# Conditioned transformer layer: value products of two key tiles at a time, four places for the probabilities, Wq and Wk resident by halves

## The chip, the cores and the metric

The kernel runs on one core of one Trainium2 chip, in one launch. The metric is device time in microseconds (us) of that core. TensorE (PE in the profile) multiplies matrices, VectorE (DVE), ScalarE (ACT) and GpSimd (POOL) work on elements, SyncE (SP) issues most transfers. Products land in eight PSUM banks of 128 x 512 floats, all else lies in SBUF.

## What is computed

```python
x = x + layer(x, cond)         # x: (4, 1024, 512) f32, cond: (4, 128)
def layer(x, t):               # 16 heads of 32
    x = x + attention(rmsnorm(x, t, g1, b1), Wq, Wk, Wv, Wo)
    return x + swiglu(rmsnorm(x, t, g2, b2), gate_w, hid_w, out_w)
def rmsnorm(x, t, gw, gb, bw, bb):
    g = (t @ gw.T + gb)[:, None, :]; b = (t @ bw.T + bb)[:, None, :]
    return g * x * rsqrt(mean(x * x, -1) + 1e-6) + b
def attention(x, Wq, Wk, Wv, Wo):
    p = softmax(einsum('blhd,bmhd->bhlm', q, k) / sqrt(32))
    return einsum('bhlm,bmhd->blhd', p, v).reshape(B, L, D) @ Wo.T
```

All is float32 in and out.

## The kernel before

`attention_program` (L241) runs first, for the four batches one after the other, then `ffn_program` (L1183) for the four. Each returns one function per engine; the engines meet only at semaphores. The change is in attention; of the feed-forward part it touches the places of tiles alone.

**Precision.** Most products are made of three with rounded parts (`product3_part`, L924): high x high, high x low, low x high. The probabilities times the values, and the denominators, are full float32 products. They have 32 columns of weights per head, so the four heads of a group run side by side in the array, and each is two instructions: a group of four heads is a row "x8" in the timeline.

**Stages of a batch.** The value stage (L1082) makes V for the eight token tiles, with the first projections and maxima woven in. Then come NU = 8 units: unit u treats head group g = u // 2 (four heads) and query half u % 2 (512 queries). In a unit TensorE goes through NS = 8 key tiles s and GH = 4 heads h; I write (s, h), or q = 4 s + h. At each (s, h) it makes one tile of scores (L1107) into one of three banks, one product for the row maxima of the next unit but a few (`max_tile`, L992, three banks, reduced by VectorE at L754), and what a table adds: a quarter of a Q or K projection (PROJECTED, L36 to L42, `project`, L958), a turned token tile of the next batch (HT_AT), the maxima's rows (MAXIMA_AT), the denominators (SUMS_AT, L46) and the values (VALUES_AT, L50). Last, eight output tiles (`out_tile`, L1019).

**The probabilities.** ScalarE writes exp of the scores (L658) to `probs`, which has places for two key tiles, s % 2. Two engines read them:

```python
46  SUMS_AT = {(5, 1): (0, 0), (1, 1): (1, 1)}
50  VALUES_AT = (3, 1, 3, 2)
498                     total = sum_place(s // QT, h)
499                     first = probs[:, 0, h, :] if s % QT == 1 else total
1123                        if h == VALUES_AT[s % QT] and (u or s):
1124                            values(b, u if s else u - 1, (s - 1) % NS)
```

GpSimd adds up each quad of four key tiles (L486 to L501): nothing at s % 4 == 0, then four sums for each of the other three tiles, in order, 24 a unit. `denominators` (L1006) on TensorE then adds over the partitions: at (5, 1) for the unit's first quad, at (1, 1) of the next unit for the second. It waits until the quad's sums are done, and GpSimd's sum at (s % 4 == 1, h = 1) waits until the denominators before it have read the places (L494). GpSimd also does the normalisation of the unit before, ahead of s = 5 (`normalise`, L460), and at (3, 6) and (6, 3) an inverse root for the next batch's norm (L456).

`values` (L1038) multiplies one key tile, four heads, and adds to the bank `obank`: tile s - 1 at (s, h) with h from VALUES_AT. The places bind ScalarE: at each s it waits until the values of tile s - 2 are done (L644), and except at s % 4 == 3 until GpSimd has taken up tile s - 2 (L654). After (0, 3) ScalarE copies the finished unit out (`output`, L582).

**The weights.** Wq, Wk (high and low part each) and Wo's low part stay in SBUF, 2048 floats per partition each. Wv's parts lie under `probs` and come back from DRAM for every batch; ScalarE issues that (L687) after the last denominators. Their rounding and splitting, `weight_hi` and `weight_lo`, is done in the lead-in on VectorE (L796 to L803), Wv's and Wo's rounding on ScalarE (L613). VectorE's splitting of Wo (L844) stands ahead of its first maxima.

**SP's queue** (L346 to L441) is in order: lead-in loads, the copies of Q and K parts stacked for the products ("stacking", 12 transfers a tile, L354), stores of Wv's and Wo's parts (L396, L398) with a wait for the latter (L399), then per unit the stackings, loads of x and of Wo.

Of the kernel before, what the change touches and what calls it, by code (L numbers as in the profile page):

```python
# [11 lines left out]
P = 128  # L12
# [37 lines left out]
VALUES_AT = (3, 1, 3, 2)  # L50
# [190 lines left out]
def attention_program(nc, ctx, x, cond_small, cond_in, W_in, attn, wv_dram, wo_dram, W, cst, psum):  # L241
# [10 lines left out]
    probs = at("probs", [P, 2, GH, QB], F32, "probs")  # L252
# [25 lines left out]
    raw = [at("wq_raw", [P, KT, D], F32, "wq_lo"), at("wk_raw", [P, KT, D], F32, "wk_lo"),  # L278
           at("wv_raw", [P, KT, D], F32, "probs_lo"), at("wo_raw", [P, KT, D], F32, "wo_lo")]
    split = [W[0], W[1], [wv[:, 0, :, :], wv[:, 1, :, :]], [wo[0], wo[1]]]  # L280
# [18 lines left out]
    wv_stored = sem("wv_stored")  # L299
    wo_stored = sem("wo_stored")  # L300
# [45 lines left out]
    def sync_part(sp, lead):  # L346
# [44 lines left out]
        sp.sem_inc(wv_loaded, 16)  # L391
# [6 lines left out]
        sp.dma_start(wo_dram, wo[0][:].bitcast(F32)).then_inc(wo_stored, 16)  # L398
        hold(sp, held, wo_stored, 16)  # L399
        def batch(b):  # L400
# [5 lines left out]
            for u in range(NU):  # L406
# [37 lines left out]
    def gpsimd_part(pool):  # L444
# [24 lines left out]
        def batch(b):  # L469
            last = isinstance(b, int)  # L470
            for u in range(NU):
                for s in range(NS):
# [13 lines left out]
                    for h in range(GH if s % QT else 0):  # L486
# [12 lines left out]
                        first = probs[:, 0, h, :] if s % QT == 1 else total  # L499
                        nc.gpsimd.tensor_tensor(total, first, probs[:, s % 2, h, :], ALU.add) \  # L500
# [7 lines left out]
    def scalar_part(act, lead):  # L508
# [104 lines left out]
        def weight_hi(w):  # L613
            act.wait_ge(w_loaded[w], 16)
            nc.scalar.activation(split[w][0][:], raw[w][:], ACT.Copy).then_inc(w_hi[w], 1)
# [11 lines left out]
        def batch(b):  # L627
            last = isinstance(b, int)
            for t in range(NT):

                act.wait_ge(st_ready, SCORES_T(b, t + 1))
                if t == 0:

                    act.wait_ge(pv_done, b * (NU * NS) + 2)
# [5 lines left out]
            for u in range(NU):  # L640
                for s in range(NS):
                    n = u * NS + s

                    act.wait_ge(pv_done, b * (NU * NS) + n + 1)  # L644
# [3 lines left out]
                    if u == 0 and s == 0:  # L648

                        act.wait_ge(wv_stored, 16)  # L650
                    for h in range(GH):
# [1307 lines left out]
```

## Time and profile before

| | |
|---|---|
| runs of the kernel | 2383.4 us median of 3 (2380.82 to 2390.84) |
| profiled execution, span of its instructions | 2384.2 us |
| the profiled execution's own time | not recorded beside its span |
| attention, four batches | to about 1372 us |
| units 0 to 7 of batch 1 | 427.85 to 701.37 us |
| TensorE, VectorE, ScalarE, GpSimd busy | 96%, 70%, 54%, 60% of the span |
| granted TensorE clock, mean | 0.989 of full speed |

The page is one profiled execution. Busy time of an engine is the time in which one of its instructions ran. Matmuls are pipelined: a row's duration overlaps the next row's, so that the distance of starts is what one costs. "Idle before <-X" says that the engine waited and whose instruction ended the wait.

### The profile page before, as it was taken

What the parts mean: (1) busy time and instruction counts of PE and PEld (TensorE: products, weight loads), DVE (VectorE), ACT (ScalarE), POOL (GpSimd) and SP (SyncE); (2) the same over time, 40 slices, a digit from 0 to 9 for tenths busy, and PEclk for the clock granted to TensorE, in tenths of its full rate; (3) what the DMA queues carried; (4) which work ended last, traced back from release to release, by engine and by line L of the source; (5) the groups of instructions that cost most, each with busy time, mean ns of one, the idle gap of its engine ahead of it and who ended that gap; (6) DMA issues with size and microseconds to landing.
All of it is one profiled execution on the core that took longest, in us unless ns stands there. A gap on an engine that the chain in (4) does not pass through costs nothing.

```text
span 2384.2 us, 38858 instructions
## 1 busy us (share of the span) xinstructions
PE 2279.8 (96%) x10848; PEld 1561.5 (65%) x10848; DVE 1658.1 (70%) x2719; ACT 1284.7 (54%) x2286; POOL 1421.4 (60%) x1331
## 2 busy tenths in 40 slices
PE   6899999999999999999999889999999999999998
PEld 5555447555457554465554468887888788888887
DVE  4777754677736777546777378877887788778877
ACT  3366672567762666735666654363436344544354
POOL 0299891699961898925999837504760466036701
PEclk9899999999999999999999999999999999999999
DMA  5321213222132222132221232046114621363125
GB/s 163 99 66 33 66 32 112 52 60 54 49 94 59 53 47 72 32 111 46 48 54 32 106 133 62 27 151 221 54 36 133 204 81 36 106 200 113 44 89 177
DMA packets 91333, 203.06 MB, mean 85 GB/s; under 512 B 15200, under 2 KB 15200, under 8 KB 89440
## 3 DMA queue, kind: packets, MB, share of 16 engines
q1 hardware_dynamic: 90672, 194.06, 27.4%
q10 hardware_dynamic: 432, 6.29, 0.7%
q8 instruction: 102, 1.67, 0.3%
q14 instruction: 127, 1.04, 0.1%
HBM read 130.03 MB, written 19.92 MB: 63 GB/s over the span
## 4 chain that ended last, share of the span: by engine, by line
PE 80%; DVE 6%; issue 5%; ACT 4%; DMA 2%; POOL 2%; SPq 2%; DVEq 0%; ACTq 0%; POOLq 0%
PE bank L1814 26%; PE bank L1828 12%; PE bank L927 10%; PE bank L1107 9%; PE bank L1046 8%; PE bank L1002 8%; PE bank L1033 3%; PE bank L1012 2%; POOL sums L500 1%; DVE pmax L754 1%; ACT probs L658 1%; SPq L365 1%; PE bank L988 1%; DMA wo_raw<-in_out_w 1%; DVE ow L1634 1%
## 5 line engine op out<-in xcount | busy, mean ns | idle before, releaser
L754 DVE TENSOR_REDUCE pmax<-bank 128x1 f32<-128x512 f32 x1024 | 651.9, 683 | 210.0 <-PE bank L1002 202.0
L658 ACT ACTIVATE probs<-bank 128x512 f32<-128x512 f32 x1024 | 566.2, 602 | 304.6 <-PE bank L1107 253.7
L500 POOL TENSOR_TENSOR sums<-sums,probs 128x512 f32<-128x512 f32 x432 | 540.7, 1287 | 0.0
L1107 PE MATMUL bank<-qs,ks 128*128 128x512 f32 x1024 | 435.6, 430 | 12.1 <-ACT probs L658 9.7
L1002 PE MATMUL bank<-ks,qs 96*128 96x512 f32 x1024 | 407.2, 410 | 30.0 <-DVE pmax L754 29.0
L1107 PEld LDWEIGHTS bank<-qs,ks 128*128 128x128 f32 x1024 | 192.7, 189 | 276.0 <-issue 130.7
L1828 PE MATMUL bank<-ow,aw 128*128 128x512 f32 x1536 | 360.8, 392 | 3.1 <-DVE ow L1634 3.0
L1814 PE MATMUL bank<-H_hi,wt_hi 128*128 128x512 f32 x896 | 350.6, 391 | 8.6 <-DVE H_lo L1669 8.3
L1814 PE MATMUL bank<-H_hi,wt_lo 128*128 128x512 f32 x896 | 350.1, 391 | 0.0
L1814 PE MATMUL bank<-H_lo,wt_hi 128*128 128x512 f32 x896 | 350.0, 391 | 0.0
L1828 PEld LDWEIGHTS bank<-ow,aw 128*128 128x128 f32 x1536 | 285.0, 188 | 65.7 <-issue 6.7
L500 POOL TENSOR_TENSOR sums<-probs 128x512 f32<-128x512 f32 x224 | 282.9, 1283 | 55.3 <-ACT probs L658 50.8
L1046 PE MATMUL bank<-probs,v 128*32 128x512 f32 x2048 | 275.1, 609 | 2.7 <-ACT probs L658 2.7
L1392 POOL TENSOR_TENSOR wt_lo<-s_ring,wt_hi 128x256 fp32r<-128x256 f32 x224 | 185.1, 859 | 151.6 <-ACT wt_hi L1459 151.6
L1002 PEld LDWEIGHTS bank<-ks,qs 96*128 96x128 f32 x1024 | 194.6, 190 | 101.3 <-DVE pmax L754 68.9
L500 POOL TENSOR_TENSOR yout<-probs 128x512 f32<-128x512 f32 x32 | 41.0, 1280 | 305.7 <-ACT probs L658 305.7
L1814 PEld LDWEIGHTS bank<-H_hi,wt_hi 128*128 128x128 f32 x896 | 169.0, 189 | 46.6 <-ACT a L1547 6.9
L1814 PEld LDWEIGHTS bank<-H_hi,wt_lo 128*128 128x128 f32 x896 | 168.9, 189 | 35.2
L1814 PEld LDWEIGHTS bank<-H_lo,wt_hi 128*128 128x128 f32 x896 | 168.9, 189 | 35.1
L1453 ACT ACTIVATE wt_hi<-raw 128x512 fp32r<-128x512 f32 x65 | 41.0, 631 | 262.7 <-PE bank L1814 262.1
L1377 POOL TENSOR_TENSOR s<-raw 128x256 f32<-128x256 f32 x9 | 7.8, 867 | 288.5 <-DVE aw L1629 288.5
L1492 ACT ACTIVATE aw<-a 128x512 fp32r<-128x512 f32 x128 | 80.4, 628 | 108.2 <-PE bank L1828 93.6
(181 smaller groups left out, 3321.4 us busy)
## 6 DMA issues: line engine op xcount, KB each, us to landing
raw<-in_gu_w SPq DMA_DIRECT2D x66, 512.0 KB, 3.6
wo_raw<-in_out_w SPq DMA_DIRECT2D x128, 256.0 KB, 2.8
qs<-qk_hi SPq DMA_DIRECT2D x256, 64.0 KB, 2.0
ks<-qk_hi SPq DMA_DIRECT2D x128, 128.0 KB, 2.4
x<-attn_out SPq DMA_DIRECT2D x10, 1024.0 KB, 8.5
x<-in_x SPq DMA_DIRECT2D x8, 1024.0 KB, 5.1
qs<-qk_lo SPq DMA_DIRECT2D x128, 64.0 KB, 2.0
ks<-qk_lo SPq DMA_DIRECT2D x64, 128.0 KB, 2.4
```

The source lines that it names most:

```text
L500: nc.gpsimd.tensor_tensor(total, first, probs[:, s % 2, h, :], ALU.add) \
L658: nc.scalar.activation(probs[:, s % 2, h, :], sbank[i % SB][:], ACT.Exp, scale=SCALE).then_inc(st_done, 1)
L754: nc.vector.reduce_max(pmax[:, t, h, hf:hf + 1], mbank[n % MB][:], AX_X).then_inc(sq_done, 1)
L927: last = nc.tensor.matmul(out, lhs(a, k), rhs(c, k), start=(k == 0 and a == 0 and c == 0), stop=(k == kdim - 1 and a == 1))
L1002: nc.tensor.matmul(mbank[n % MB][:], qs[0:96, u % 3, h, t * P:(t + 1) * P], ks[0:96, u // 2 % 2, h, hf * QB:(hf + 1) * QB], start=True, st ...
L1033: last = nc.tensor.matmul(bank[:], osplit[:, t % 2, a, k, :], wo[c][:, k, :], start=(k == 0 and a == 0 and c == 0), stop=(k == NG - 1 and ...
L1046: last = nc.tensor.matmul(obank[DH * h:DH * h + DH, :], v[:, s, (g * GH + h) * DH:(g * GH + h + 1) * DH], probs[:, s % 2, h, :], start=(s ...
L1107: nc.tensor.matmul(sbank[i % SB][:], ks[:, g % 2, h, s * P:(s + 1) * P], qs[:, u % 3, h, :], start=True, stop=True).then_inc(st_ready, 1)
L1392: nc.gpsimd.tensor_tensor(lo[:, S1 + i], src[:, i], hi[:, S1 + i].bitcast(F32), ALU.subtract).then_inc(s_lo, 1)
L1492: nc.scalar.activation(aw[n % 3][:, 0, :], a[:, j, blk, :], ACT.Copy).then_inc(a_hi, 1)
L1814: last = nc.tensor.matmul(bank[:], wt[j % 2][p][:, weight, i, :], H[q][:, h, i, :], start=(i == 0 and p == 0 and q == 0), stop=(i == 1 and ...
L1828: last = nc.tensor.matmul(psum[4 * blk + t][:], aw[n % 3][:, p, t * P:(t + 1) * P], ow[n % 3][:, q, :], start=(j == 0 and p == 0 and q == ...
```

## The change

1. The values of two key tiles are multiplied in one go, four times a unit: tiles 0 and 1 at (3, 1), 2 and 3 at (5, 1), 4 and 5 at (7, 1), 6 and 7 at (1, 1) of the next unit, there and at (5, 1) right behind the denominators.
2. `probs` has four places, s % 4. ScalarE waits for values only at even s, for the pair two before, and for sums four tiles back. `output` moves from (0, 3) to (1, 1), the copying of the first denominators from (5, 2) to (5, 1).
3. The space for that: Wq and Wk are held for two of four head groups. The lead-in splits groups 0 and 1 first, 2 and 3 later (into space that the probabilities use afterwards), and SP stores all parts to DRAM. In each batch SP reloads each group over one that is done with (`load_group`, eight loads of 512 KB, six of them placed by unit; in the last batch only the four of units 0 and 1). Projections wait for the loads.
4. Wv's reload is issued by ScalarE after the last exponential instead of after the last denominators.
5. Places of some feed-forward tiles are exchanged.

```diff
-VALUES_AT = (3, 1, 3, 2)
+PAIRS = NS // 2
+VALUES_AT = {(3, 1): (0, 0), (5, 1): (0, 1), (7, 1): (0, 2), (1, 1): (1, 3)}
...
+    def probs(s, h):
+        return probs_parts[s % 4 // 2][:, s % 2, h, :]
...
+        def load_group(b, kind, g):
+
+            last_user = ("Q", 2 * g + 1) if kind == "Q" else ("K", 2 * g, NHALF - 1)
+            to, dram, loaded = (wq, wq_dram, wq_loaded) if kind == "Q" else (wk, wk_dram, wk_loaded)
+            hold(sp, held, w_ready, MISC(b, 0 if last_user == ("K", 0, NHALF - 1) else misc_index(b, last_user) + 1))
+            hold(sp, held, loaded, b * (NG * 16) + 16 * (g + 1))
+            sp.dma_start(to[:, g % 2, :, :, :].bitcast(F32), dram[(g + 2) % NG]).then_inc(loaded, 16)
...
         hold(sp, held, w_hi[3], 1)
         sp.dma_start(wo_dram, wo[0][:].bitcast(F32)).then_inc(wo_stored, 16)
+        for w, (dram, lower) in enumerate(((wq_dram, wq), (wk_dram, wk))):
+            for half, part in enumerate((lower, upper[w])):
+                hold(sp, held, w_lo[w], half + 1)
+                sp.dma_start(dram[2 * half:2 * half + 2].rearrange("g p a k c -> p g a k c"),
+                             part[:].bitcast(F32)).then_inc(qk_stored, 16)
         hold(sp, held, wo_stored, 16)
...
                     stack(b, ("Q", u + 2), (u + 2) % 3)
+                if u == 0:
+                    hold(sp, held, qk_stored, 64)
+                    load_group(b, "Q", 0)
+                    load_group(b, "K", 0)
+                elif u == 1:
+                    load_group(b, "Q", 1)
+                    load_group(b, "K", 1)
+                elif u < 6 and not last:
+                    load_group(b, "K" if u % 2 == 0 else "Q", u // 2 + 1)
...
-                    act.wait_ge(pv_done, b * (NU * NS) + n + 1)
+                    if s % 2 == 0:
+                        act.wait_ge(pv_done, b * (NU * PAIRS) + n // 2 + 1)
...
-                        if s % QT != QT - 1:
-
-                            act.wait_ge(sum_done, sums_done(b, u, s - 2, h) if s >= 2
-                                        else sums_done(b, u - 1, NS + s - 2, h))
-                        nc.scalar.activation(probs[:, s % 2, h, :], sbank[i % SB][:], ACT.Exp,
+                        if s % QT != 1:
+
+                            act.wait_ge(sum_done, sums_done(b, u, s - QT, h) if s >= QT
+                                        else sums_done(b, u - 1, NS + s - QT, h))
+                        nc.scalar.activation(probs(s, h), sbank[i % SB][:], ACT.Exp,
...
-                        if (s, h) == (5, 2):
+                        if (s, h) == (5, 1):
                             work_tile(b, ("D", u, 0))
...
-                        if (s, h) == (0, GH - 1) and u:
+                        if (s, h) == (1, 1) and u:
                             output(b, u - 1)
...
+                        if (u, s, h) == (NU - 1, NS - 1, GH - 1) and not last:
+
+                            act.wait_ge(pv_done, b * (NU * PAIRS) + NU * PAIRS + 1)
+                            act.wait_ge(sum_done, sums_done(b, u, 5, GH - 1))
+                            act.dma_start(wv[:].bitcast(F32), wv_dram).then_inc(wv_loaded, 16)
...
         for hf in range(NHALF):
             work_tile(None, ("K", 0, hf))
+        for w in range(2):
+            weight_hi(w, 1)
+            weight_lo(w, 1)
         weight_lo(3)
...
-        def values(b, u, s):
+        def values(b, u, pair):
 
             g = u // 2
-            pe.wait_ge(st_done, SCORES_T(b, NT + (u * NS + s + 1) * GH) + SB)
-            if s == 0:
+            pe.wait_ge(st_done, SCORES_T(b, NT + (u * NS + 2 * pair + 2) * GH) + SB)
+            if pair == 0:
 
                 pe.wait_ge(od_act, b * NU + (u + 1))
-            for h in range(GH):
-                last = nc.tensor.matmul(obank[DH * h:DH * h + DH, :], v[:, s, (g * GH + h) * DH:(g * GH + h + 1) * DH],
-                                        probs[:, s % 2, h, :], start=(s == 0), stop=(s == NS - 1))
+            for s in (2 * pair, 2 * pair + 1):
+                for h in range(GH):
+                    last = nc.tensor.matmul(obank[DH * h:DH * h + DH, :], v[:, s, (g * GH + h) * DH:(g * GH + h + 1) * DH],
+                                            probs(s, h), start=(s == 0), stop=(s == NS - 1))
             last.then_inc(pv_done, 1)
...
                         if sums_at(u, s, h):
                             denominators(b, *sums_at(u, s, h)[1:])
-                        if h == VALUES_AT[s % QT] and (u or s):
-                            values(b, u if s else u - 1, (s - 1) % NS)
-            values(b, NU - 1, NS - 1)
+                        back, pair = VALUES_AT.get((s, h), (NU, 0))
+                        if u >= back:
+                            values(b, u - back, pair)
+            values(b, NU - 1, PAIRS - 1)
```

## Rows read from the trace of the kernel before

**Rows 1.** The page, part 5, the largest group of sums on GpSimd (POOL)

```profile
L500 POOL TENSOR_TENSOR sums<-sums,probs 128x512 f32<-128x512 f32 x432 | 540.7, 1287 | 0.0
```

**Rows 2.** Timeline of TensorE, batch 3, into unit 6: start, us, what, [idle before <-releaser]

```profile
1290.00 0.40 PE L1002 MATMUL bank<-ks,qs 96*128 96x512 f32 x1
1290.33 1.06 PE L1046 MATMUL bank<-probs,v 128*32 128x512 f32 x8
1291.33 0.50 PE L1107 MATMUL bank<-qs,ks 128*128 128x512 f32 x1
1291.66 0.40 PE L1002 MATMUL bank<-ks,qs 96*128 96x512 f32 x1
...
1292.14 0.40 PE L1002 MATMUL bank<-ks,qs 96*128 96x512 f32 x1
1294.11 1.06 PE L1012 MATMUL bank<-sums,ones 128*32 128x512 f32 x8 [1.57 <-POOL sums L500]
1294.96 1.07 PE L1046 MATMUL bank<-probs,v 128*32 128x512 f32 x8
1295.96 0.50 PE L1107 MATMUL bank<-qs,ks 128*128 128x512 f32 x1
```

**Rows 3.** Timeline of GpSimd over the same stretch

```profile
1293.91 1.28 POOL L500 TENSOR_TENSOR yout<-probs 128x512 f32<-128x512 f32 x1
...
1297.17 2.52 POOL L500 TENSOR_TENSOR sums<-probs 128x512 f32<-128x512 f32 x2 [0.55 <-ACT probs L658]
```

**Rows 4.** By stage, batch 1: length, PE, PEld, DVE, ACT, POOL busy, clock, DMA

```profile
427.85:452.07 24.22, 23.30 (x108) 13.79 (x106) 17.75 (x28) 13.71 (x25) 15.02 (x13) 1.00 0.36 79
452.07:469.59 17.52, 17.28 (x90) 9.39 (x90) 12.44 (x24) 12.06 (x22) 14.92 (x12) 1.00 0.12 29
469.59:485.65 16.06, 16.06 (x85) 8.84 (x84) 12.85 (x22) 9.24 (x19) 15.43 (x13) 1.00 0.41 115
485.65:502.56 16.91, 16.82 (x89) 9.26 (x88) 11.51 (x22) 12.28 (x23) 15.72 (x13) 1.00 0.00 1
502.56:519.49 16.93, 16.59 (x86) 8.83 (x85) 12.92 (x22) 9.26 (x19) 16.23 (x13) 1.00 0.49 107
...
552.47:569.41 16.94, 16.85 (x89) 9.27 (x89) 12.07 (x25) 12.76 (x24) 16.73 (x14) 1.00 0.00 0
569.41:588.31 18.90, 17.45 (x89) 9.12 (x88) 13.58 (x23) 12.93 (x25) 16.21 (x13) 1.00 0.54 120
...
605.23:621.88 16.65, 15.39 (x85) 7.78 (x85) 13.84 (x24) 12.30 (x24) 16.02 (x13) 1.00 0.39 108
621.88:637.51 15.63, 14.12 (x78) 6.98 (x77) 11.50 (x22) 12.80 (x25) 15.17 (x14) 1.00 0.20 71
637.51:654.40 16.89, 16.42 (x85) 8.74 (x85) 12.15 (x21) 10.35 (x23) 16.20 (x14) 1.00 0.01 2
654.40:670.43 16.03, 12.99 (x77) 6.12 (x77) 4.78 (x11) 15.19 (x28) 15.83 (x13) 1.00 0.13 30
670.43:689.33 18.90, 17.87 (x94) 9.89 (x93) 6.92 (x11) 15.84 (x30) 15.31 (x13) 1.00 0.16 36
689.33:701.37 12.04, 11.35 (x67) 5.74 (x70) 1.29 (x2) 7.47 (x14) 9.77 (x8) 1.00 0.47 104
...
898.66:918.56 19.90, 18.74 (x89) 9.55 (x88) 13.57 (x23) 12.96 (x25) 16.25 (x14) 0.91 0.54 120
```

**Rows 5.** Timelines of VectorE, SyncE and TensorE in the lead-in and first value stage

```profile
19.61 1.22 DVE L798 CAST wk_hi<-wk_raw 128x2048 fp32r<-128x2048 f32 x1
...
62.95 0.32 SPq L398 DMA_DIRECT2D wo_part<-wo_hi  x1
...
66.43 1.39 PE L1002 MATMUL bank<-ks,qs 96*128 96x512 f32 x2 [13.97 <-DVE pmax L754]
...
83.80 0.39 PE L927 MATMUL bank<-hT_hi,wk_hi 128*128 128x512 f32 x1
```

**Rows 6.** The DMA issues by line: KB each, median us from issue to landing

```profile
wv_parts<-wv SPq DMA_DIRECT2D x1, 2048.0 KB, 11.2
```

More of the change, by code:

```diff
@@ L277, in attention_program, with split, whole @@
     gwT = at("gwT", [P, 4, D], F32, "cond_w")
-    raw = [at("wq_raw", [P, KT, D], F32, "wq_lo"), at("wk_raw", [P, KT, D], F32, "wk_lo"),
+    raw = [at("wq_raw", [P, NG, KT, P], F32, "sums"), at("wk_raw", [P, NG, KT, P], F32, "o_up"),
            at("wv_raw", [P, KT, D], F32, "probs_lo"), at("wo_raw", [P, KT, D], F32, "wo_lo")]
-    split = [W[0], W[1], [wv[:, 0, :, :], wv[:, 1, :, :]], [wo[0], wo[1]]]
+    upper = [at("wq_up", [P, 2, 2, KT, P], F32R, "probs_up"), at("wk_up", [P, 2, 2, KT, P], F32R, "wk_up")]
+    def split(w, part, half):
+        if w < 2:
+            return ((wq, wk)[w] if half == 0 else upper[w])[:, :, part, :, :]
+        return (wv[:, part, :, :], wo[part][:])[w - 2]
+    def whole(w, half):
+        return raw[w][:, 2 * half:2 * half + 2, :, :] if w < 2 else raw[w][:]
     sbank = psum[0:SB]
@@ L650, in batch @@
                         act.wait_ge(wv_stored, 16)
+                    if u == 0 and s == 2:
+                        act.wait_ge(qk_stored, 64)
                     for h in range(GH):
@@ L969, in project @@
             g = tile[1] // 2 % NG
+            if b is not None and k == 0 and tile != ("Q", 1):
+                order = NG if tile[1] == NU else g
+                pe.wait_ge(wq_loaded if tile[0] == "Q" else wk_loaded, b * (NG * 16) + order * 16)
             hf = tile[1] % 2 if tile[0] == "Q" else tile[2]
-            product3_part(work_bank(b, tile)[:], lambda a, k: w[a][:, k, g * P:(g + 1) * P],
+            product3_part(work_bank(b, tile)[:], lambda a, k: w[:, g % 2, a, k, :],
                           lambda c, k: hT[c][:, k, hf * QB:(hf + 1) * QB], k, KT, w_ready)
@@ L1014, in denominators @@
             for h in range(GH if direct else 0):
-                last = nc.tensor.matmul(wbank[DH * h:DH * h + DH, :], ones[:], probs[:, (NS - 1) % 2, h, :], start=False,
+                last = nc.tensor.matmul(wbank[DH * h:DH * h + DH, :], ones[:], probs(NS - 1, h), start=False,
                                         stop=True)
@@ L1844, in condition_block @@
     wo_dram = nc.dram_tensor("wo_part", (P, KT, D), F32, kind="Internal").ap()
+    wq_dram, wk_dram = (nc.dram_tensor(f"{n}_parts", (NG, P, 2, KT, P), F32, kind="Internal").ap() for n in ("wq", "wk"))
     base = (nc.sbuf_base + 31) // 32 * 32
-    WEIGHTS = ("wq_hi", "wq_lo", "wk_hi", "wk_lo", "wo_lo")
     def plan(start, regions):
@@ L1858, in condition_block @@
     const_at, base = plan(base, small)
[L1859 removed]
+    weights_at, after_weights = plan(base, [("wq", KT * D), ("wk", KT * D), ("wo_lo", KT * D), ("probs_up", 2 * GH * QB)])
     attention_at, _ = plan(after_weights, [
@@ L1890, in condition_block @@
     cst["g1"], cst["b1"], cst["g2"], cst["b2"] = cst["cond"]
-    parts = [at(n, [P, KT, D], F32R, n) for n in WEIGHTS]
-    W = [parts[0:2], parts[2:4], parts[4]]
+    W = [at(n, [P, 2, 2, KT, P], F32R, n) for n in ("wq", "wk")] + [at("wo_lo", [P, KT, D], F32R, "wo_lo")]
     with ExitStack() as ctx:
         psum = [ctx.enter_context(nc.psum_tensor(f"bank{i}", [P, QB], F32)) for i in range(8)]
-        attention, ends = attention_program(nc, ctx, x, cond_small, cond_w, w_in, attn, wv_dram, wo_dram, W, cst, psum)
+        attention, ends = attention_program(nc, ctx, x, cond_small, cond_w, w_in, attn, wv_dram, wo_dram, wq_dram, wk_dram, W, cst, psum)
         ffn = ffn_program(nc, ctx, x, attn, gu_w, out_w, out, ends, cst, psum)
```

47 lines of the change are left out of this document (26 added, 21 removed).

## The prediction, made before the changed kernel was run

> **What bounds the kernel now.** I read the page's busy shares first: TensorE is busy 96% of the 2384.2 us span, and no other engine is over 70% (the table above). That is a mean over two programs. The change touches only the first, attention (to about 1.37 ms), so I cut one batch of it into stages. In program order the natural cut is the pair of points in each unit where TensorE issues the denominators' products (`denominators`, L1006): head 1 of key tile 1 and of key tile 5. I call the stretch from one such start to the next a half: A ends at tile 5, B at tile 1 of the next unit, and each has 16 scores. The table by stage of batch 1 [rows 4] gives a length, the busy time of each engine and the granted clock for every half.
>
> The reader is to see two things there. First, most halves are nearly full on TensorE: 16.06 of 16.06 us busy in A of units 1 and 3, 16.8 of 16.9 in B of units 1, 2 and 4. Second, GpSimd is not the relaxed engine that its 60% suggests. It is busy 14.9 to 16.7 us in each half but the last, and from unit 5 on TensorE has holes (14.12 of 15.63 us, 12.99 of 16.03) while GpSimd has nearly none. One sum costs 540.7 / 432 = 1.25 us back to back [rows 1], and there are 12 in a half, plus one normalisation (L465) per unit.
>
> The timelines of a half's beginning in batch 3 show who waits for whom. GpSimd is through with the sums that they need at 1293.91, where the next one starts [rows 3]; TensorE, idle for 1.57 us, starts the denominators at 1294.11 [rows 2]. GpSimd goes on with the sum of head 0, whose exponentials are there, then head 1, and is then idle for 0.55 us until 1297.17, for head 2's exponential: its score could only be issued after the burst of narrow products, at 1295.96. So a **recurrence** closes: denominators, burst, next score (1.85 us), exponential (sum at 3.06 us), ten sums from there on, some 0.1 us of latency, next denominators. 3.06 + 12.5 + 0.1 = 15.7 us, and B of unit 5 in batch 1 has 15.63 [rows 4]. I take 15.63 as the floor; TensorE-bound ones are only 0.4 to 1.3 us above it.
>
> **The change, part by part.**
>
> *Switches.* A lone value burst: the maxima product before it starts at 1290.00, the next score at 1291.33 [rows 2]. Without the burst these starts would be 0.24 apart (1291.66 to 1292.14 is two products). It streams in 0.86 us, which is what the values add when they stand behind the denominators: 1295.96 - 1294.11 = 1.85, of which 1294.96 - 1294.11 = 0.85 is the denominators. With the 0.10 us by which the score after a burst is long (0.50 against 0.40), entering and leaving cost 1.33 - 0.24 - 0.86 + 0.10 = 0.33 us. Per unit there are eight bursts before and four after; the streaming is unchanged. That is 4 x 32 x 0.33 = 42.2 us off TensorE, 0.66 per half.
>
> *The burst behind the denominators gets longer.* Before, they are followed by one tile's values; afterwards by two, 0.86 us more (same rows). The next score comes at 2.71 instead of 1.85 and the exponential that GpSimd waits for ends at 3.06 + 0.86 = 3.92 to 4.0. `output` now also stands ahead of that exponential on ScalarE (after head 1 of tile 1); it waits for the burst's end and takes 0.5 of ScalarE's pitch, ready just as the score is, so I give it 0 to 0.1. Its cover was a burst; there is none now. GpSimd gets nothing in exchange: its order and waits are the same, and four places don't let it pass the denominators' gate. So its floor for a half goes from 15.63 to **16.5 us**. Where a normalisation fell into the gap (B halves) it still fits: normalisation and two sums are 3.75 us, under 4.0.
>
> *Four places.* Exponentials no longer wait for sums two tiles back. The page's kind of wait is in the first half of unit 0 (0.5 us, an estimate from 24.22 against 23.30 busy [rows 4]) and in A of unit 5 (TensorE busy 15.39 of 16.65 us, over the floor by 1.0). They go; behind them stands GpSimd's floor.
>
> *Halves, before to after* [rows 4]; TensorE's own time is the row less 0.66, except where noted, and the larger of it and the floor stands. Unit 0: 24.22 to 22.7 (three switches and the 0.5); 17.52 to 16.8. Units 1 to 3, A: 16.06 to 16.5 in units 1 and 3, 16.93 to 16.6 in unit 2. B: 16.91 to 16.5, in units 1 and 2 alike. B of unit 3, 16.94, has an inverse root on GpSimd (L458; 14 operations and 16.73 us busy against 13 and 15.72): floor 17.5. Unit 4: 18.90 to 18.3, for its stalls are VectorE's and ScalarE's (turned tokens, normalisation) and eight scores in a row leave them less relief; B as in units 1 and 2, to 16.5. Unit 5: 16.65 to 16.5; 15.63 to 16.5. Unit 6: 16.89 to 17.5 (inverse root again); 16.03 to 16.5. Unit 7: 18.90 to 18.3, 12.04 to 11.6. The sum goes from 273.5 to 271.3: **-2.2 us a batch**, of which +3.35 are halves that get longer. Batches 0 and 2 are alike. Batch 3 has no projections or roots for a next one; five of its halves are already near the floor (15.6 to 16.1) and grow, and I work out -1.3. Together -7.9.
>
> *Lead-in.* VectorE rounds and splits only two head groups of Wq and Wk early: each rounding is 1.22 us [rows 5] and becomes half, which lets the turned tokens' low parts start up to 1.1 us earlier; everything to the end of TensorE's 13.97 us wait at 66.43 hangs on that chain. -1.1 (0 to -2.3). The other halves run in VectorE's hole before Wo arrives, four operations of some 3.5 us together, behind which nothing waits; without that cover they would cost their length once. SP gets four 1 MB stores behind Wo's, ahead of its wait and of the stacking of Q1. 2 MB took 11.2 us with another transfer in its way [rows 6], so 5 MB from 62.95 on [rows 5] are done at 91 by that row, and at 77 if they go twice as fast; Q1's stacked copies land behind them. ScalarE wants those for the K projection that TensorE begins at 83.80 and ends 2.7 us later (12 products). I take 0, nearer to the faster end since Wo's load shared that row, with +5 as the bound.
>
> *Reloads.* Eight transfers of 512 KB per batch on SP, each behind stackings already issued and ahead of those of a unit later; what they wait for has long happened. A quarter of the size of [rows 6], well under 11 us, and a unit or more before its use: 0, bounds 0 and +1 a batch from slower stackings. Wv's reload is issued by ScalarE one step earlier, under the last burst; its new waits are already over: 0. The semaphore waits at the projections: 0.
>
> The profile's sum is 2384.2 - 7.9 - 1.1 = 2375.2 us. The execution is 0.8 us above the runs' median of 2383.4, far inside their 10 us, so I forecast **2375**, -0.35%.
>
> **A rule weighed.** Four halves of all (one of them is batch 2's A of unit 4, 19.90 us at a mean clock of 0.91, against 18.90 at 1.00 in batch 1 [rows 4]) show TensorE at its lower clock, 1.2 GHz, for a few us, 1.0 us lost each. TensorE had been busy 18.74 of those 19.90 us, with no long hole. The Trainium skill, "TensorE: Matmul & The Clock Gate", section "Why this matters for your kernels", asks only that long idle gaps between bursts be avoided. By it the waits of about 1 us that I add cost nothing and the sum stays at 2375; by the row a thin stretch may do it.
>
> **Rivals.** *TensorE alone decides.* Then all 42.2 us show and it is 2340. For: 96% busy, waits on GpSimd in few halves. Against: the recurrence matches a row. The Trainium skill, "TensorEngine Tiling (Array Packing)", section "Key Properties", says that changing the tiling mode drains the engine; by that rule each change of mode saved is worth the same wherever it stands, which is this rival. *The floor stays at 15.63*, because the exponentials for GpSimd come early enough in some way I don't see: then each half is its row less 0.66, or 15.7, units 5 and 6 stay, -8.5 a batch, 2349.
>
> *Slower: the clock.* TensorE will wait 0.3 to 1.2 us before most denominators and then run a narrow burst. If the lower clock is granted after that, each time costs 1.0 us (same pair of halves). Four such times exist now; above 21 more it is slower by over 0.5%. In every second of the 62 halves it gives 2375 + 31 = 2406. Against: the 1.57 us wait [rows 2] and B of unit 5 (14.12 of 15.63 busy, clock 1.00) had none.
>
> **How the numbers follow.** Forecast 0.72, TensorE alone 0.05, floor unchanged 0.10, clock 0.13. The forecast's own range is 2366 to 2384 (lead-in, reloads, half of the halves 0.1 off). For 8 in 10 I reach towards the others: 2359 to 2392. A measurement of this kernel can tell about 0.5%, 12 us, from no change. 2371.5 lies inside the forecast's range: of its 0.72 some 0.22 are below it; with the two fast rivals that is 0.37 faster. 0.49 same; 0.14 slower.
>
> **What would show it.** Right: halves of 16.5 us in units 1 to 6, nearly equal; TensorE idle before L1012 for GpSimd in most of them, and GpSimd idle some 1.4 us for the exponential of head 2, ending 4.0 us after the denominators' start. ScalarE's waits for sums gone. Wrong: halves of 15.4 to 16.2 with TensorE full, or GpSimd's gap unchanged at 0.5; a clock of 0.9 in many halves; ScalarE waiting for a stacking in batch 0's value stage.

## The result and the profile after

The changed kernel takes 2405.1 us (median of 4 runs, 2403.0 to 2406.0), the kernel before 2382.1 (4 runs; the table ahead has the 2383.4 of three of them): a ratio of **1.0098** (1.0084 to 1.0112), 23.0 us slower. I had forecast 2375 us and a range up to 2392. The profiled execution's span is 2402.7 us against 2384.2, and these 18.5 us lie as follows: attention from the first score of batch 0 to the last denominators of batch 3, 1284.6 us against 1259.4 (+25.2); the lead-in 4.0 us shorter; all behind attention 2.7 us shorter.

That one window in both kernels (length, then PE, PEld, DVE, ACT and POOL busy with their instructions, mean granted clock, DMA share, GB/s), of the kernel before:

```profile
94.75:1354.14 1259.39, 1209.24 (x6122) 683.80 (x6124) 805.82 (x1394) 779.33 (x1396) 974.83 (x787) 0.99 0.23 61
```

and of the changed one:

```profile
90.78:1375.36 1284.58, 1192.65 (x6122) 698.27 (x6123) 797.40 (x1394) 778.17 (x1396) 976.61 (x788) 0.99 0.26 71
```

TensorE's busy time fell by 16.6 us, and its idle time rose from 50.2 to 91.9 us. So the question is what it waits for. Batch 1 by stage, the halves that answer to [rows 4], in order B0, A1, B1, A2, B2, B3, B4, A5, B5, A6, A7, B7 (A is the half from (1, 1) to (5, 1) of a unit, B from there to (1, 1) of the next):

```profile
449.95:467.68 17.73, 16.80 (x90) 9.62 (x89) 12.08 (x24) 11.98 (x20) 14.47 (x13) 1.00 0.30 90
467.68:484.23 16.55, 16.20 (x84) 9.03 (x84) 12.71 (x22) 9.71 (x19) 14.88 (x13) 1.00 0.61 174
484.23:501.22 16.99, 16.20 (x88) 9.59 (x89) 11.46 (x23) 11.80 (x21) 16.44 (x14) 1.00 0.01 3
501.22:517.85 16.63, 16.29 (x84) 8.94 (x84) 12.36 (x21) 9.36 (x19) 14.89 (x13) 1.00 0.48 104
517.85:534.99 17.14, 16.21 (x90) 9.59 (x89) 11.48 (x23) 12.02 (x21) 16.24 (x14) 1.00 0.26 70
...
551.54:568.99 17.45, 16.19 (x89) 9.57 (x88) 12.32 (x27) 13.43 (x25) 17.19 (x15) 1.00 0.00 1
...
587.45:605.43 17.98, 17.05 (x89) 9.62 (x88) 11.03 (x22) 11.94 (x21) 14.73 (x13) 0.96 0.14 41
605.43:622.62 17.19, 15.38 (x85) 7.93 (x85) 13.73 (x23) 12.49 (x24) 15.52 (x13) 1.00 0.44 123
622.62:639.04 16.42, 13.75 (x78) 7.05 (x77) 11.64 (x23) 12.48 (x24) 15.47 (x14) 1.00 0.22 81
639.04:658.16 19.12, 17.86 (x84) 9.14 (x84) 12.45 (x22) 11.47 (x24) 15.95 (x14) 0.91 0.01 2
...
674.64:695.80 21.16, 18.97 (x93) 10.27 (x93) 6.93 (x11) 15.30 (x30) 15.08 (x12) 0.93 0.09 20
695.80:709.55 13.75, 12.73 (x83) 6.36 (x86) 1.29 (x2) 8.09 (x15) 10.05 (x8) 1.00 0.59 132
```

A of units 1 and 2 and B of unit 5 are at the forecast 16.5 us, up from 16.06 and 15.63 in A1 and B5. But B of units 1, 2 and 4 is no shorter than before (16.9), though each holds two bursts less (and so two times entering and leaving), and A5, A7 and B7 grew.

The beginning of A of unit 2 shows both sides. TensorE:

```profile
501.22 1.06 PE L1065 MATMUL bank<-sums,ones 128*32 128x512 f32 x8 [0.56 <-DVE qk_lo L792]
502.10 1.91 PE L1100 MATMUL bank<-probs_up,v 128*32 128x512 f32 x16
503.93 0.50 PE L1161 MATMUL bank<-qs,ks 128*128 128x512 f32 x1
...
506.15 0.40 PE L1055 MATMUL bank<-ks,qs 96*128 96x512 f32 x1
506.39 0.39 PE L1161 MATMUL bank<-qs,ks 128*128 128x512 f32 x1
506.65 0.50 PE L1055 MATMUL bank<-ks,qs 96*128 96x512 f32 x1
506.99 0.40 PE L1161 MATMUL bank<-qs,ks 128*128 128x512 f32 x1
507.25 0.50 PE L1055 MATMUL bank<-ks,qs 96*128 96x512 f32 x1
```

and GpSimd:

```profile
500.93 1.28 POOL L539 TENSOR_TENSOR yout<-probs 128x512 f32<-128x512 f32 x1 [0.29 <-ACT probs L701]
502.39 1.28 POOL L539 TENSOR_TENSOR sums<-probs 128x512 f32<-128x512 f32 x1 [0.19 <-PE bank L1065]
505.23 1.29 POOL L539 TENSOR_TENSOR sums<-probs 128x512 f32<-128x512 f32 x1 [1.55 <-ACT probs L701]
```

The next score comes 2.71 us after the denominators' start and GpSimd's sum of head 2 at 4.01, both as forecast. Two things are not. The denominators waited 0.56 us for VectorE, which had not yet emptied the work bank of a K tile (`qk_lo`). And from 506.15 us on the maxima products start 0.50 and 0.60 us apart and the score at 506.99 comes 0.60 after its predecessor, where TensorE alone needs 0.47: 0.60 is the pace of VectorE's reductions of the maxima.

Nor does TensorE wait for GpSimd before most of the denominators, as my list of signs had it. The waits of these products, ended by GpSimd and by VectorE (us in total, times, longest), are these, for 64 starts:

```profile
PE bank L1065 <- POOL sums L539: 26.1, 16, 3.3
PE bank L1065 <- DVE qk_lo L792: 10.3, 16, 0.7
```

In batches 0 to 2 GpSimd ends a wait at the end of B3, B5 and A6 alone; seven of its sixteen are in batch 3. Waits too short for this count can still bind a half: A1 is on the floor without one.

### The profile page after: what moved, and what is told of

It is laid out like the page before. It is cut to its first block, busy times and chain, and to the rows that moved or that the text cites. A ratio compares the mean times of both kernels' runs of the same rounds, so it can differ in the third digit from the quotient of the medians.

```text
span 2402.7 us, 38915 instructions
## 1 busy us (share of the span) xinstructions
PE 2257.4 (94%) x10848; PEld 1571.5 (65%) x10848; DVE 1651.2 (69%) x2723; ACT 1283.7 (53%) x2286; POOL 1420.6 (59%) x1331
## 4 chain that ended last, share of the span: by engine, by line
PE 46%; DVE 4%; issue 3%; POOL 1%; ACT 1%; DMA 1%; SPq 0%; DVEq 0%; ACTq 0%; POOLq 0%
PE bank L1869 25%; PE bank L1883 12%; PE bank L976 2%; PE bank L1100 2%; POOL sums L539 1%; PE bank L1086 1%; PE bank L1055 1%; PE bank L1161 1%; DVE pmax L800 1%; PE bank L1065 1%; DVE ow L1689 1%; PE bank L1837 1%; DVE aw L1684 1%; DVE x L1694 1%; DMA wo_raw<-in_out_w 0%
## 5 line engine op out<-in xcount | busy, mean ns | idle before, releaser
L539 POOL TENSOR_TENSOR sums<-sums,probs_up 128x512 f32<-128x512 f32 x432 | 540.5, 1287 | 0.0
L1055 PE MATMUL bank<-ks,qs 96*128 96x512 f32 x1024 | 420.8, 422 | 32.6 <-DVE pmax L800 30.8
L1161 PE MATMUL bank<-qs,ks 128*128 128x512 f32 x1024 | 421.8, 417 | 14.5 <-ACT probs L701 7.8
L701 ACT ACTIVATE probs<-bank 128x512 f32<-128x512 f32 x512 | 286.3, 602 | 105.4 <-PE bank L1161 101.7
L701 ACT ACTIVATE probs_up<-bank 128x512 f32<-128x512 f32 x512 | 282.6, 605 | 101.0 <-PE bank L1161 96.2
```

The source lines that it names most:

```text
L539: nc.gpsimd.tensor_tensor(total, first, probs(s, h), ALU.add) \
L701: nc.scalar.activation(probs(s, h), sbank[i % SB][:], ACT.Exp, scale=SCALE).then_inc(st_done, 1)
L1055: nc.tensor.matmul(mbank[n % MB][:], qs[0:96, u % 3, h, t * P:(t + 1) * P], ks[0:96, u // 2 % 2, h, hf * QB:(hf + 1) * QB], start=True, st ...
L1161: nc.tensor.matmul(sbank[i % SB][:], ks[:, g % 2, h, s * P:(s + 1) * P], qs[:, u % 3, h, :], start=True, stop=True).then_inc(st_ready, 1)
```

## The experiments

Twelve kernels; six of them fill a table with the two kernels of the change. The kernel before took 2382.9 us beside e1 to e4, 2382.0 beside e5 to e8, 2381.9 beside e9 to e11, 2381.1 beside e12. `VALUES_AT` is written {where it is issued: (units back, pair)}.

**e1, values first.** The pair is issued ahead of the denominators at the two points where both stand.

```diff
+                        back, pair = VALUES_AT.get((s, h), (NU, 0))
+                        if u >= back:
+                            values(b, u - back, pair)
                         if sums_at(u, s, h):
                             denominators(b, *sums_at(u, s, h)[1:])
-                        back, pair = VALUES_AT.get((s, h), (NU, 0))
-                        if u >= back:
-                            values(b, u - back, pair)
```

> Edit of the changed kernel: where both stand at one place, TensorE issues the pair of value products before the denominators instead of after them. Nothing else moves. Theory (gate and cover): the long burst hurts because it stands between the denominators, which GpSimd's next sums wait for, and the next score; and because the denominators, issued right after a projection, wait for its bank. With the values ahead, GpSimd's idle time after the denominators goes from 1.5 to under 0.3 us, its floor for a half from 16.4 to about 14.9 us, the wait of 0.6 us for qk_lo at (1, 1) vanishes, and halves are 15.3 to 16.5 us, bound by TensorE. Some 9 us a batch and part of the falls of the clock: 2355 to 2370 us. Rival (four places, reloads or the lower clock cost the time): the order changes nothing, 2400 to 2408 us.

2371.9 us, ratio 0.9956 (0.9940 to 0.9971): 33 us faster than the changed kernel, faster than the kernel before, and 2 us above the range expected. B of units 1 and 5 (both ends are starts of denominators, so the swap shifts them alike; only unit 0's first half looks a burst longer by it and B7 a burst shorter):

```profile
477.41:493.77 16.36, 16.13 (x92) 9.65 (x88) 11.30 (x21) 11.71 (x20) 15.89 (x13) 1.00 0.00 1
...
611.94:626.85 14.91, 13.86 (x80) 6.99 (x72) 10.32 (x20) 12.59 (x24) 13.87 (x13) 1.00 0.19 71
```

The floor fell from 16.4 to 14.9: in e1 GpSimd goes on 1.16 us after the denominators' start, and eleven sums follow (13.75 us). At the end of B1 the burst now runs while VectorE empties the bank: the slot (1, 1) takes 3.28 us instead of 3.90. One edit takes two waits away, so the time of e1 alone doesn't divide them; its trace does. TensorE waits 9.2 us for GpSimd before the denominators instead of 26.1, and no longer for the bank (10.3 before). And its busy time in attention is 10.8 us lower (1181.9 for 1192.7), mostly since the lower clock is granted once there instead of 7 times.

**e2, the same swap in the kernel before.**

> Edit of the kernel before: the same exchange of order, with its one tile of values. Theory (gate): only halves that sit on GpSimd's floor of 15.63 gain, down to 14.9 or to TensorE's own time: three halves a batch and five in the last, some 0.7 us each, so 2370 to 2378 us against 2382. Rival (the order is immaterial, TensorE is the bound everywhere): 2382 within 2 us.

2383.3 us, ratio 1.0001 (0.9989 to 1.0013): a miss, the rival's time. B5 fell to 14.91 as expected, but the next halves of batch 1 took it back (B6 rose from 16.03 to 18.04, at a mean clock of 0.91, and GpSimd waited 2.6 us in it for an exponential). The order is worth something only where the floor lies above the rest, and before it hardly did.

**e3, single tiles with all else.** Four places, the reloads and the shorter lead-in stay; one tile at a time at the old points, output at the old place.

```diff
-VALUES_AT = {(3, 1): (0, 0), (5, 1): (0, 1), (7, 1): (0, 2), (1, 1): (1, 3)}
+VALUES_AT = (3, 1, 3, 2)
...
-                        if (s, h) == (1, 1) and u:
+                        if (s, h) == (0, GH - 1) and u:
                             output(b, u - 1)
```

> Edit of the changed kernel: four places, reloads, stores, lead-in and the earlier reload of Wv stay, but values are multiplied one key tile at a time at the old points, and output is copied at the old point. Theory (only the pairs cost): as before or better, by the shorter lead-in (first score 4 us earlier) and the exponentials' waits that go: 2374 to 2383 us. Rival (places or reloads cost, by slower stackings or contention): 2390 us or more.

2375.8 us, ratio 0.9972 (0.9959 to 0.9985). So places, stores and reloads cost nothing, and **the pairing costs 29 us**, with the output copy moved along with it. Some 9 of the 29 are the lower clock, an estimate from the 1.5 us that one time costs (below): it is granted once in e3's attention and 7 times in the changed kernel.

**e4, the second point one head later.** SUMS_AT, VALUES_AT and output: (1, 2) for (1, 1).

> Edit of the changed kernel: the denominators and the pair of values at (1, 1), and the output copy, stand one head later, at (1, 2), so that 0.47 us more lie between the projection's last product and the denominators that need its bank. Theory (cover): TensorE's wait for qk_lo goes from 0.56 to 0.69 us to 0.1 to 0.2, and the halves of units 1 to 4 that end there from about 17.0 to 16.5 us, GpSimd's floor; -6 to -9 us, 2396 to 2400. Rival (that wait lies on nothing because GpSimd's floor is behind it): 2405 within 2 us.

2388.6 us, ratio 1.0025 (1.0013 to 1.0037), 16.5 us less than the changed kernel and twice what I expected. Half of it is the wait for the bank, as I had it, and half the wait for GpSimd, which I hadn't expected:

```profile
PE bank L1065 <- POOL sums L539: 16.9, 11, 2.8
PE bank L1065 <- DVE qk_lo L792: 2.0, 9, 0.2
```

GpSimd has one more sum at hand during the burst. An A half now has one slot of 0.47 us less and a B half one more; in unit 5 of batch 3 the two together take 31.85 us instead of 33.04. So the floor depends on where the points are placed; it is no property of the pair.

**e6, e1 and e4 together.** If e4's gain is that of waits which e1 takes away too, nothing is left to gain on e1.

> The changed kernel with both edits of e1 and e4: the pair of values ahead of the denominators, and the unit's second such point (with output) one head later, at head 2 of tile 1. In e1 the floor was gone (GpSimd waits 0.3 us for TensorE), so a later point has no floor to give way to. Theory: e4's 16.5 us were the floor's alone, so on top of e1 it gives at most 3 us: 2368 to 2374. Rival: e4's gain came from something else than the floor (the work bank turned over during one more score, or VectorE's relief), then it adds here too, 8 us or more: 2355 to 2364.

2375.9 us, ratio 0.9973 (0.9964 to 0.9983), 4 us more than e1 and 2 above the theory's range, far from its rival: A1 and A2 fall by 0.6 us and B1 and B2 rise by 0.45, which is the slot that moved. So e4's gain came from waits that e1 takes away too. The floor and the bank are both among these, so e6 doesn't divide them.

**e5, pairs apart from the denominators.** Six bursts per unit; the denominators alone at their points.

```diff
-VALUES_AT = {(3, 1): (0, 0), (5, 1): (0, 1), (7, 1): (0, 2), (1, 1): (1, 3)}
+VALUES_AT = {(2, 3): (0, 0), (4, 3): (0, 1), (6, 3): (0, 2), (0, 3): (1, 3)}
...
-                        if (s, h) == (1, 1) and u:
+                        if (s, h) == (0, GH - 1) and u:
```

> The changed kernel with the pairs taken away from the denominators: pair 0 after head 3 of tile 2, pair 1 after head 3 of tile 4, pair 2 after head 3 of tile 6, pair 3 after head 3 of tile 0 of the next unit; output back behind tile 0. Six bursts per unit instead of four, but the one behind which GpSimd waits holds the denominators alone, there is a burst again between the K or Q tile's last product and the denominators, and no longer eight scores in a row twice in each unit without relief from both. Theory (what the change lost is the long burst at the denominators, the lost cover and the runs of scores; the saved switches are real): two switches fewer per unit than before, 32 x 0.66 = 21 us, the floor of a half 14.9 or less in unit 5 (B 15.63 to about 14.9), batch 1's A of units 1 and 3 about 15.7 instead of 16.06, B of units 1 and 2 about 16.3 instead of 16.91, lead-in gain kept: 2352 to 2366 us. Rival (pairs make VectorE late wherever they stand, as eight scores follow each other between tiles 2 and 4 and between 4 and 6): halves as long as before, 2370 to 2378. Rival (pairing itself costs, by four places or longer bursts of any kind): 2385 or more.

2409.1 us, ratio 1.0119 (1.0100 to 1.0139): the worst of all, and my largest miss. A1 is at 15.68 and B5 at 15.05 as expected, but B1 takes 17.74. TensorE at the end of tile 7 of unit 1:

```profile
496.13 1.92 PE L1100 MATMUL bank<-probs,v 128*32 128x512 f32 x16
497.98 0.50 PE L1161 MATMUL bank<-qs,ks 128*128 128x512 f32 x1
...
499.73 0.40 PE L1055 MATMUL bank<-ks,qs 96*128 96x512 f32 x1
501.00 0.47 PE L1161 MATMUL bank<-qs,ks 128*128 128x512 f32 x1 [0.87 <-ACT probs_up L701]
```

and ScalarE:

```profile
496.24 1.02 ACT L581 ACTIVATE qs<-bank 32x1024 fp32r<-32x1024 f32 x1 [0.41 <-PE bank L1041]
498.60 0.60 ACT L701 ACTIVATE probs_up<-bank 128x512 f32<-128x512 f32 x1 [1.34 <-PE bank L1161]
499.22 1.02 ACT L581 ACTIVATE qs<-bank 32x1024 fp32r<-32x1024 f32 x1
500.26 1.58 ACT L701 ACTIVATE probs_up<-bank 128x512 f32<-128x512 f32 x3
```

ScalarE copies the rows of the maxima in two pieces of 1.02 us, the second behind the first exponential of tile 7. The burst ahead of tile 7 delays that exponential (ScalarE idle for 1.34 us), then the three banks of scores are full during the copy, and TensorE stops. In the changed kernel a burst comes behind (7, 1), and ScalarE catches up under it.

**e9, the same with two bursts moved back** to the changed kernel's places.

```diff
-VALUES_AT = {(3, 1): (0, 0), (5, 1): (0, 1), (7, 1): (0, 2), (1, 1): (1, 3)}
+VALUES_AT = {(3, 1): (0, 0), (4, 3): (0, 1), (7, 1): (0, 2), (0, 3): (1, 3)}
```

(and output as in e5)

> e5 again with two of its four bursts elsewhere: the pair that e5 had after head 3 of tile 6 back after head 1 of tile 7, and the one that it had after head 3 of tile 2 back after head 1 of tile 3, both as in the changed kernel. e5's trace shows TensorE stopped for 1.04 us at head 3 of tile 7 in 28 of its units (the slot takes 1.51 us instead of 0.47): the burst stands before the scores of tile 7, so ScalarE gets to the second eviction of the row maxima (1.02 us) only when three scores are already in the banks. Theory (a burst is also the time in which ScalarE and VectorE catch up, so its place decides): that stop goes in every unit, 28 x 1.04 = 29 us, and with it some of the 3 to 4 us in A of unit 5 (19.79 and 17.83 us): 2368 to 2382, B of unit 1 at 16.7 or less. Rival (pairs away from the denominators are bad wherever they stand): 2395 or more.

2375.4 us, ratio 0.9969 (0.9955 to 0.9983): 34 us by moving two bursts. A1 and B1:

```profile
464.22:480.16 15.94, 15.94 (x86) 8.84 (x85) 12.82 (x22) 9.35 (x19) 15.79 (x13) 1.00 0.58 181
480.16:496.87 16.71, 16.47 (x90) 9.47 (x89) 11.41 (x22) 12.24 (x23) 15.31 (x13) 1.00 0.02 5
```

So pairs are harmless apart from the denominators, if their places suit ScalarE. e9 moved both bursts at once; the 1.0 us of B halves is (7, 3)'s stop, A of unit 5 (16.65 for 17.83) is the other's or both's. Part of the 34 us is the lower clock: 4 times in e9's attention, 12 in e5's.

**e7 and e8, halved reductions of the maxima** in the changed kernel and in the kernel before. Each maximum is taken over the first 256 of its 512 columns, that is over half of the keys; this leaves out half of VectorE's reading.

```diff
-            nc.vector.reduce_max(pmax[:, t, h, hf:hf + 1], mbank[n % MB][:], AX_X).then_inc(sq_done, 1)
+            nc.vector.reduce_max(pmax[:, t, h, hf:hf + 1], mbank[n % MB][:, 0:QB // 2], AX_X).then_inc(sq_done, 1)
```

> The changed kernel in which each of the 1024 max reductions reads the first 256 of its 512 columns, so that the maximum of each query is taken over half of the keys; all else is as it was. It takes VectorE's pitch (0.60 us a reduction) out of the runs of scores. Theory (eight scores in a row go at VectorE's pitch of 0.60 instead of TensorE's 0.47, and slots (2,3), (3,0), (4,3), (5,0), (6,3) are late by it; the wait for qk_lo at the unit's start shrinks too, as VectorE comes to it sooner): A of units 2, 5, 6 and 7 in batch 1 fall from 16.63, 17.18, 19.13 and 21.16, A of units 1 and 3 and B of unit 5 stay at GpSimd's 16.4 to 16.55: 8 to 14 us in all, 2389 to 2397, and more than twice what the kernel before gains by the same edit (e8). Rival (GpSimd's floor alone decides): 2401 to 2405, no more than e8 gains.

> The kernel before with the same halved reductions, as the measure for e7. Theory: single bursts already give VectorE its relief, most halves are TensorE's own, so 0 to 5 us: 2378 to 2383. Rival (VectorE's reductions hold TensorE back in both alike): both gain the same, 8 us or more here too, 2375 or less.

2389.3 us (ratio 1.0032, 1.0021 to 1.0043) and 2360.2 us (0.9913, 0.9893 to 0.9932). The changed kernel gained 15.8 us, a little more than expected; the kernel before gained 21.8, far more. e8's rival, that VectorE holds back both kernels, holds: before, it is late in unit 0 and in A of units 4 and 5. What e7 shows besides is my forecast's picture, clean (A1, B1, A2, B2, then A5, B5):

```profile
459.54:476.09 16.55, 15.83 (x84) 9.24 (x84) 9.85 (x23) 9.66 (x19) 14.89 (x13) 1.00 0.60 168
476.09:492.55 16.46, 15.88 (x88) 9.65 (x88) 7.10 (x20) 11.77 (x20) 16.20 (x14) 1.00 0.03 9
492.55:509.10 16.55, 15.84 (x84) 9.18 (x84) 9.74 (x23) 9.48 (x19) 15.00 (x13) 1.00 0.48 105
509.10:525.66 16.56, 15.87 (x88) 9.65 (x88) 7.00 (x20) 11.65 (x20) 16.29 (x14) 1.00 0.27 72
593.03:609.53 16.50, 15.11 (x84) 8.01 (x84) 10.52 (x25) 12.66 (x24) 14.84 (x13) 1.00 0.46 123
609.53:625.93 16.40, 13.15 (x76) 7.29 (x76) 7.23 (x21) 12.20 (x24) 16.14 (x14) 0.99 0.24 86
```

Six halves of quite different content, all at 16.4 to 16.56: that is GpSimd's floor. TensorE waits for GpSimd at the end of five of them; B2 ends with the wait for the bank.

**e10 and e11, both brakes out**: e1 and e2, each with the halved reductions.

> e1 (values ahead of the denominators) with e7's halved max reductions: both brakes out, GpSimd's wait for the next score and VectorE's pitch. Theory: now the switches show. e7 had A halves at GpSimd's 16.55 and B halves at 16.5; here A of units 1 to 3 should be 15.2 to 15.6 and B 16.1 to 16.4, a unit of 31.5 against 32.9 in e8, of which GpSimd's own work (24 sums and a normalisation of 1.25 us, 31.3 us) allows no more. 2322 to 2338, and 30 to 40 us under e11. Rival (pairing gives nothing even then, since what it saves is lost in the same places): 2348 to 2360, within 10 us of e11.

> e2 (the kernel before with the values ahead of the denominators) with the same halved reductions, as the measure for e10. e8 gained 22 us by them and e2 nothing by the swap; theory: 2355 to 2363. If VectorE's pitch was what hid the swap's gain in e2: 2345 to 2353.

2325.9 us (ratio 0.9763, 0.9742 to 0.9784) and 2356.4 us (0.9885, 0.9864 to 0.9907). Here the whole change gives **30.5 us**, of which some 6 may be its other parts, by e3. A1 and B1 of e10:

```profile
445.53:461.33 15.80, 15.74 (x89) 9.26 (x85) 9.17 (x21) 9.61 (x18) 14.73 (x13) 1.00 0.63 183
461.33:477.12 15.79, 15.79 (x93) 9.56 (x88) 7.61 (x21) 11.62 (x20) 15.79 (x14) 1.00 0.00 1
```

31.59 us a unit against 32.86 in e8 and 33.01 in e11: 1.27 and 1.42, and my 4 x 0.33 were 1.32. The saved switches are real. Together (us); the right column has all parts of the change:

| | single tiles | pairs |
|---|---|---|
| denominators first | 2382.1 (before) | 2405.1 (after) |
| values first | 2383.3 (e2) | 2371.9 (e1) |
| denominators first, halved maxima | 2360.2 (e8) | 2389.3 (e7) |
| values first, halved maxima | 2356.4 (e11) | 2325.9 (e10) |

With single tiles the swap gives nothing and 4 us. With pairs the swap gives 33 us, and 63 once VectorE is out of the way: the two brakes cover each other.

**e12, maxima products placed by VectorE's pace**, on e1, in search of more.

```diff
-MAX_END = 25
+MAX_END = 24
...
+for u in range(1, NU - 1):
+    MAX_AT[u * UNIT + 2] += 1
+    MAX_AT[u * UNIT + 10] -= 1
```

> e1 with the maxima products placed by VectorE's pitch: the 32 products of a unit end one slot earlier (in unit 0 they are spread over 24 slots instead of 25), and in units 1 to 6 one product is taken from head 2 of tile 2 and issued at head 2 of tile 0, where projection products stand and VectorE has time. The arithmetic is that of e1. In e1's trace TensorE loses 0.50 us before the turning of the maxima (head 3 of tile 6 takes 1.49 us against 0.97 in e7), and about 0.13 us in each of three slots from head 3 of tile 2 on. Theory (those are VectorE's pitch and its queue): head 3 of tile 6 falls to 1.0 to 1.1 us and the three slots to 0.47 (or 1.16 with projections), unit 0 gets 0.6 us longer; 2.5 to 4.5 us a batch, 10 to 18 us: 2354 to 2362, faster than both kernels. Rival (GpSimd's 25 operations a unit bound e1 just behind): 2366 to 2371.

2381.6 us, ratio 0.9998 (0.9989 to 1.0007): 20 us above the range expected, and 10 more than e1's 2371.9. A1 fell (16.48 to 15.99), B1 rose (16.36 to 16.86). TensorE of e12 at (6, 3) of unit 1:

```profile
486.15 0.40 PE L1164 MATMUL bank<-qs,ks 128*128 128x512 f32 x1
487.16 0.50 PE L1058 MATMUL bank<-ks,qs 96*128 96x512 f32 x1 [0.60 <-DVE pmax L803]
487.49 0.61 PE L1044 MATMUL bank<-identr,mt 128*128 128x128 f32 x4
```

The wait for the transposed maxima is gone as wished, and the same engine is waited for at the product before, longer: VectorE does its four closing operations one reduction earlier, then has no empty bank to give. An earlier due time doesn't help when the queue behind it is full. But that is the smaller part. Attention is 15.2 us longer than in e1 in the profiled executions, and 9.0 of them are TensorE's busy time: the lower clock is granted 10 times there, once in e1. Why isn't shown: of the waits of 1.8 us and more, which go with it elsewhere (below), attention has one in e12 and two in e1. No version here that reads the whole maxima beats e1.

## Why the prediction was wrong

*The switches: right.* 0.33 us each by e10. *The floor: right in its terms and size* (2.71 and 4.01; 16.4 to 16.56 in e7's rows), but it ends fewer halves than I said: A1 takes 16.55 us in the changed kernel and 16.48 in e1, where the floor is 1.5 lower. e1 and e4 lower it and gain 33 and 16.5 us, together with the bank's wait and, in e1, the clock. *Four places, stores, reloads: right*, nothing (e3); ScalarE's waits for sums went as I said. *The lead-in: right in sign*, -4.0 for -1.1. I didn't test it, and the first score moves by 2.5 us among kernels that share this lead-in (90.59 in e4, 93.10 in e9).

*What failed is the step "Halves, before to after"*, in its sentence that TensorE's own time is the row less 0.66 and the larger of it and the floor stands. That gave -2.2 us a batch. Where no half is slowed by the clock (batch 2 after, 278.2 us, against batch 1 before, 273.5) it is +4.7. The 6.9 us between are:

- B0, B1, B2 and B4 are 0.5 to 0.9 us over forecast, 2.9 in all. The lone burst at (0, 3) used to cover the emptying of the work bank before the denominators at (1, 1). I priced eight bursts as cost alone and didn't ask what ran under each. I did name such covers, but for output and not for the bank. In the trace it is the wait for `qk_lo`, 0.56 us above; neither e1 nor e3, which has the burst at (0, 3), shows it.
- A7 +1.4 is the same: a lone burst at (2, 3) used to stand between two K projections in unit 7. Now the second finds the work bank full (batch 2), as in e1, e7, e9, e10 and e12, and not in e3:

```profile
1019.76 0.47 PE L976 MATMUL bank<-hT_hi,wk 128*128 128x512 f32 x1 [1.45 <-DVE qk_lo L792]
```

- A5 +0.7, unit 0's first half +0.6, A4 -0.6: without single bursts between them eight scores follow each other, and VectorE's 0.60 us a reduction decides instead of 0.47. I saw that for unit 4 ("less relief") and not that it holds for every run of scores. Halved reductions take 1.25 us off A1 and B1 together in the kernels with pairs and values first (32.84 in e1, 31.59 in e10), and 0.11 off the kernel before (32.97, 32.86 in e8). They bring A5 to 16.50, the forecast; 0.56 us of waiting for ScalarE's exponential are new in A5 too, and stay.
- B7 +2.15 (13.75 against 11.6). A plain miscount: between the last unit's (5, 1) and its last denominators stand six tiles' values now, and four before. So two tiles' values, 1.72 us, move from the first half of a batch to its end (TensorE's instructions there go from 67 to 83, in the first half from 108 to 91), and unit 0, held by VectorE, doesn't get shorter by as much.

*The rest is the clock*, my slower rival, which was right in kind and too dear. TensorE runs at its lower level (1.2 GHz) in more places than before. A of unit 6 took 19.12 us at a mean of 0.91 in batch 1 and 17.51 at 1.00 in batch 2; A of unit 7 21.16 and 19.65; in batch 3 that half has 0.85. In this order, A6 and A7 of batch 2 and A7 of batch 3:

```profile
976.06:993.57 17.51, 16.23 (x85) 8.94 (x85) 12.47 (x22) 11.44 (x24) 15.95 (x14) 1.00 0.01 2
1010.03:1029.68 19.65, 17.42 (x92) 10.15 (x92) 6.92 (x11) 15.32 (x30) 15.07 (x12) 1.00 0.11 25
1340.70:1360.01 19.31, 15.49 (x65) 5.99 (x66) 4.44 (x7) 11.34 (x22) 14.90 (x13) 0.85 0.46 171
```

Ahead of A6 of batch 1 stands this wait:

```profile
636.19 0.50 PE L1055 MATMUL bank<-ks,qs 96*128 96x512 f32 x1
639.04 1.06 PE L1065 MATMUL bank<-sums,ones 128*32 128x512 f32 x8 [2.34 <-POOL sums L539]
```

I had called waits of 0.3 to 1.2 us; in unit 5, with no projections, they are 2.3. Each such stretch costs 1.5 to 1.6 us (these pairs), not the 1.0 that I took, but there are 7 in attention against 4, not 31: some 5 us of the 23. So it is luck that the rival's 2406 is nearly the 2405 measured. Do the waits bring the lower clock? Five of the 7 begin within 1.1 us of the end of one of the eight waits of 1.9 us and more; the other two don't, and three such waits have none. e7, where TensorE waits for GpSimd at most points, has 13; e10 has 3. But e12 has 10 with one such wait. So the waits are likely one cause and not the only one; no run tests it.

In sum, batch by batch (first score to last denominators): forecast -2.2, -2.2, -2.2, -1.3; measured +2.5, +9.4, +3.6, +9.9. The batches differ mostly by the clock: before, the four batches have 2, 0, 1 and 1 of the times at the lower level, and after, 1, 3, 0 and 3. Four times 6.9 us and the clock's 5 are 33, what attention as a whole was off by (+25.2 for -7.9); for batch 3, which has no projections, the 6.9 is an estimate.

As to the rule weighed in the prediction, "TensorE: Matmul & The Clock Gate", "Why this matters for your kernels" in the Trainium skill (avoid long idle gaps between bursts): the lower clock followed a gap of 2.34 us here, which is on its side, yet in the kernel before it came in a half in which TensorE was busy for 18.74 of 19.90 us [rows 4], and there the rule would not have it. The rule of the rival *TensorE alone*, in the Trainium skill's "TensorEngine Tiling (Array Packing)", "Key Properties", that a change of mode drains the engine, fits the price of a switch, 0.32 to 0.36 us by e10 against e8 and e11. My reading of it, that each is worth the same wherever it stands, doesn't hold: in the changed kernel TensorE's busy time fell by 16.6 us and its idle time rose by 41.7.

## What to carry to other kernels

A short piece of work on the busiest engine may be what lets the others catch up. Before you merge or move it, list for each instance what ends under it (a bank emptied, a copy, a reduction) and price that as new waits; count how many items then follow each other without a pause, and hold their pace against that of every engine that serves them. Where two bursts stand at one point and another engine waits for one of them and then for the first score behind both, put the one that it doesn't wait for first: here this swap was worth 33 us, and turned a change that costs 1% into one that gains 0.4%.

## What the runs showed of the hardware

- A reduction of 128 x 512 from PSUM to a column goes at 0.60 us a piece on VectorE (the starts of the products that wait for it: 506.65 and 507.25 us above). With 256 columns (e7) TensorE waits 3.7 us for the reductions in attention instead of 18.1.
- GpSimd's sums keep 1.25 us each next to whatever VectorE does: its busy time in the window of attention is 974.8 us before, 975.3 in e7 and 973.9 in e10, with VectorE at 806, 572 and 570 us.
- With both brakes out, B1 of e10 has TensorE busy 15.79 and GpSimd busy 15.79 of 15.79 us. Little is left in this design: 25 operations of 1.25 us on GpSimd are 31.3 us a unit, and this one takes 31.6.
